# A graph network on one core: four instead of three tiles a batch gathered by matrix products in two of its passes, with the gather's table in six blocks of 128 rows and a stacked rest

## The reference

```python
def _L2_gnn_ref(inputs, timestamp, W, b, src, dst):          # pass 7
    msg = inputs[src] * timestamp
    h = jax.ops.segment_max(msg, dst, num_segments=inputs.shape[0])
    return h @ W.T + b

def _L3_gnn_ref(hx, edgefeats, edge_src, edge_dst, fnet_w1, fnet_b1, fnet_w2, fnet_b2, ...):
    w = jax.nn.relu(edgefeats @ fnet_w1 + fnet_b1) @ fnet_w2 + fnet_b2
    W = w.reshape(-1, nc, nc)
    for _ in range(NREPEATS):                                # two rounds: passes 8 and 9
        xj = hx[edge_src]
        m = jnp.einsum('ei,eio->eo', xj, W)
        agg = jax.ops.segment_sum(m, edge_dst, num_segments=n_nodes)
        agg = agg * inv_deg[:, None]
        hx = _gru_cell(agg, hx, gru_w_ih, gru_w_hh, gru_b_ih, gru_b_hh)
    return hx

x = _layernorm(x + _L0_gnn_ref(...)); x = _layernorm(x + _L1_gnn_ref(...))
x = _layernorm(x + _L2_gnn_ref(...)); x = _layernorm(x + _L3_gnn_ref(...))
```

## Time and profile before

| | |
|---|---|
| Time, median of 3 runs | 9585.77 us (9583.65 to 9609.09) |
| Profiled execution | 9624.08 us, span 9622.1 us |
| Busy over the span | PE 91%, PEld 66%, DVE 73%, ACT 38%, POOL 51% |
| Granted TensorE clock, mean | 0.915 |
| Pass 7, 8, 9 begin with the table's load at about | 4758, 6609, 8108 us |
| Indirect fetches of passes 7 to 9 (L657) | 3030, mean 970 ns |
| Products of `gather8` (L711) | 12726, mean 343 ns, overlapping |
| One-hot comparisons (L1457) | 4242, mean 316 ns |

### The profile page before, as it was taken

How to read it: one execution, slowest core, us unless ns; L and a number is a source line. 1 busy time by engine, 2 the same in 40 slices (tenths; PEclk the granted TensorE clock), 3 DMA queues, 4 the chain that set the end, 5 groups by cost and what they waited for, 6 DMA issues and landing times.

```text
span 9622.1 us, 208480 instructions
## 1 busy us (share of the span) xinstructions
PE 8789.0 (91%) x72187; PEld 6327.8 (66%) x72191; DVE 7010.4 (73%) x13550; ACT 3702.5 (38%) x10806; POOL 4954.2 (51%) x4703
## 2 busy tenths in 40 slices
PE   1599999999976999997699999998999998999998
PEld 0366666666524975976477777776777776777776
DVE  2488899999742123122378777777999998999998
ACT  5245444444320002000144444444555554555554
POOL 0588788788750000000175555544777663777662
PEclk9999999999955987987689888888999998999998
DMA  8633333333218864967732222222222221222221
GB/s 303 234 92 101 115 105 105 104 104 103 71 58 338 326 240 185 345 239 283 270 65 65 64 64 64 64 64 47 54 54 53 53 54 42 53 54 54 53 54 36
DMA packets 869111, 1162.86 MB, mean 121 GB/s; under 512 B 269846, under 2 KB 751298, under 8 KB 868118
## 3 DMA queue, kind: packets, MB, share of 16 engines
q1 hardware_dynamic: 674612, 1078.18, 33.9%
q0 software_dynamic: 150336, 28.94, 3.7%
q10 hardware_dynamic: 43426, 45.70, 1.5%
HBM read 1018.14 MB, written 133.22 MB: 120 GB/s over the span
## 4 chain that ended last, share of the span: by engine, by line
PE 66%; DVE 17%; issue 7%; DMA 5%; SPq 4%; ACT 1%; DVEq 0%; ACTq 0%
PE ps L830 16%; PE ps L711 14%; PE ps L909 9%; PE ps L700 6%; DMA arena<-adj 5%; PE ps L788 4%; PE ps L847 3%; SPq L576 3%; DVE arena L1995 3%; DVE dinv L1995 3%; PE ps L720 2%; DVE dinv L1457 2%; DVE invdeg L1457 2%; PE ps L983 2%; PE ps L795 2%
## 5 line engine op out<-in xcount | busy, mean ns | idle before, releaser
L657 POOL DMA_INDIRECT arena<-tab,x_all x3030 | 2939.7, 970 | 3700.1 <-DMA tab<-stage 2239.4
L675 POOL DMA_INDIRECT adj<-acc x1616 | 1960.8, 1213 | 560.2 <-issue 471.5
L909 PE MATMUL ps<-arena 128*128 128x192 bf16 (+1 forms) x16464 | 1167.9, 234 | 172.0 <-DMA arena<-adj 171.3
L909 PEld LDWEIGHTS ps<-arena 128*128 128x128 bf16 x16464 | 1118.2, 103 | 229.8 <-DMA arena<-adj 198.7
L711 PE MATMUL ps<-dinv,acc 112*128 112x384 bf16 x6363 | 1163.8, 342 | 44.0 <-DVE acc L1485 43.5
L1105 ACT ACTIVATE wide<-ps,not_all 128x256 bf16<-128x256 f32 x1616 | 741.0, 485 | 1197.3 <-PE ps L795 1197.3
L711 PE MATMUL ps<-invdeg,acc 112*128 112x384 bf16 x6363 | 1173.7, 344 | 2.8 <-issue 2.8
L1277 ACT ACTIVATE arena<-w_iota,rel 128x128 f32<-128x128 f32 x3232 | 988.8, 388 | 13.1
L711 PEld LDWEIGHTS ps<-dinv,acc 112*128 112x128 bf16 x6363 | 642.1, 104 | 523.7 <-issue 182.3
L711 PEld LDWEIGHTS ps<-invdeg,acc 112*128 112x128 bf16 x6363 | 645.0, 105 | 492.4 <-issue 155.4
L1621 DVE TENSOR_TENSOR arena<-hot_a,threes 128x1024 bf16<-128x1024 bf16 x606 | 738.4, 1218 | 0.0
(11 more groups left out here) (314 smaller groups left out, 14116.1 us busy)
## 6 DMA issues: line engine op xcount, KB each, us to landing
arena<-adj SPq DMA_DIRECT2D x588, 896.0 KB, 6.9
x_all<-src_parts SPq DMA_DIRECT2D x606, 192.0 KB
arena<-rels SPq DMA_DIRECT2D x202, 512.0 KB
arena<-tab SPq DMA_DIRECT2D x1616, 64.0 KB
adj<-zero SPq DMA_DIRECT2D x28, 3136.0 KB, 27.5
arena<-rT SPq DMA_DIRECT2D x404, 128.0 KB
arena<-tab,x_all POOLq DMA_INDIRECT x3030
adj<-acc POOLq DMA_INDIRECT x1616
```

The costliest lines, as they stand in the source:

```text
L657: pool.indirect_dma_start(G[b][:, u, :], None, TABLE[PHASES[p]], bass.IndirectOffsetOnAxis(ap=idx[:, t:t + 1], axis=0)).then_inc(gathered[ ...
L675: pool.indirect_dma_start(adj_cells, bass.IndirectOffsetOnAxis(ap=pair[:, t, 0:1], axis=0), pair16[:, t, 2:3], None).then_inc(celled[g], 16)
L909: last = mm(ps[:, 2 * par + u // 2, u % 2 * W:(u % 2 + 1) * W], ring[i][:, s, u * P:(u + 1) * P], rows[:, j * SC + s, :, :].rearrange("p k ...
```

## The change

In passes 8 and 9 PE gathers 4 tiles and POOL fetches 4; in pass 7 it stays at 3 and 5 (`by_pe`, `by_pool`, `skipped`, where pass 7 leaves out the first of the four tiles' columns). The table is cut into 6 blocks of 128 rows; the 16 rows left over (`LEFT`) of all three pieces are stacked at partitions 0, 32 and 64 and share one product. So `gather8` has 6 times 3 plus 1 = 19 products, of 384 columns in pass 7 and 512 in passes 8 and 9; `hot_rows` keeps 7 comparisons, now over 128 lanes, of 384 or 512 columns. The table's load is one DMA plus three small ones, and the cut has two more small copies on DVE. `src_parts` and its broadcast loads grow from 3 to 4 tiles in all three passes. Line numbers in the diff are not the profile's.

```diff
-GT = 3
+GT = 4
-FETCHED = HT - GT
-BLANES = NB8 // BL
+BLANES = P
+LAST = BL - 1
+LEFT = NB8 - LAST * BLANES
+STACKED = 3 * 32
+def by_pe(p, k):
+    return GT - 1 if p == 7 else GT
+def by_pool(p, k):
+    return HT - by_pe(p, k)
+def skipped(p, k):
+    return GT - by_pe(p, k)
...
# SyncE, start of a pass
-                sp.dma_start(x8_whole, tab_blocks).then_inc(x8_in, 16)
+                sp.dma_start(x8_whole[:, 0:LAST, :], tab_blocks).then_inc(x8_in, 16)
+                if p == 7:
+                    sp.wait_ge(left_open, 1)
+                for i in range(3):
+                    sp.dma_start(x8_whole[32 * i:32 * i + LEFT, LAST, :], tab_left).then_inc(x8_in, 16)
...
# POOL, gather_rows
-                for u in range(FETCHED):
+                for u in range(by_pool(p, k)):
...
# PE, gather8
-                for b in range(BL):
+                lo = skipped(p, j) * P
+                for b in range(LAST):
                     for i in range(3):
-                        last = mm(picked_rows, x8[:, b, i, :], hot8[j % 2][:, b, :],
-                                  start=b == i == 0, stop=b == BL - 1 and i == 2)
+                        mm(picked_rows[:, lo:], x8[:, b, i, :], hot8[j % 2][:, b, lo:], start=b == i == 0, stop=False)
+                last = mm(picked_rows[:, lo:], x8[0:STACKED, LAST, 0, :], hot8[j % 2][0:STACKED, LAST, lo:],
+                          start=False, stop=True)
...
# PE, turn8
-                for u in range(GT):
+                for u in range(skipped(p, j), GT):
...
# DVE, hot_rows
+                lo = skipped(p, j) * P
                 for b in range(BL):
-                    last = ts(hot8[j % 2][:, b, :], parts_row[j % SL][0:BLANES, 0:GC], lane_b[0:BLANES, b:b + 1], None,
+                    last = ts(hot8[j % 2][:, b, lo:], parts_row[j % SL][0:BLANES, lo:GC], lane_b[0:BLANES, b:b + 1], None,
                               ALU.is_equal)
...
# DVE, select8
-                stt(picked_by[j % 2], parts_row[j % SL][:, GC:], lane_a[:, 0:1], picked_rows, ALU.is_equal, ALU.mult
+                lo = skipped(p, j) * P
+                stt(picked_by[j % 2][:, lo:], parts_row[j % SL][:, GC + lo:], lane_a[:, 0:1], picked_rows[:, lo:],
+                    ALU.is_equal, ALU.mult
...
# DVE, open_select
+                dve.wait_ge(x8_cut, at + 4)
+                for i in (1, 2):
+                    nc.vector.tensor_copy(x8[32 * i:32 * i + 32, LAST, 0, :], x8[32 * i:32 * i + 32, LAST, i, :]
+                                          ).then_inc(x8_cut, 1)
```

More of the change, by code:

```diff
@@ L172, in build @@
         hot8 = [(dinv if i == 0 else invdeg)[0:BLANES, o:o + BL * GC // 2].bitcast(bf16).rearrange("p (b e) -> p b e", b=BL)
-                for i, o in enumerate((HOT8, 5120))]
+                for i, o in enumerate((HOT8, 4864))]
         src_g, src_t = [x_all[0:T // TR, 1664 + i * 2 * GC:1664 + (i + 1) * 2 * GC].bitcast(i32) for i in range(2)]
         src_16 = [x_all[0:T // TR, 1664 + (4 + i) * GC:1664 + (5 + i) * GC].bitcast(f16) for i in range(2)]
-        PARTS0 = 1664 + 6 * GC
+        PARTS0 = 1664
         parts_row = [x_all[:, PARTS0 + i * GC:PARTS0 + (i + 1) * GC].bitcast(f16) for i in range(SL)]
-        CONST0 = PARTS0 + SL * GC
+        CONST0 = 1664 + 6 * GC
         lane_b, lane_a = x_all[:, CONST0:CONST0 + BL], x_all[:, CONST0 + 8:CONST0 + 9]
@@ L280, in build @@
         src_parts = nc.dram_tensor("src_parts", [T // HT, 2, GC], f16).ap()
-        tab_blocks = tab16.rearrange("(b l a) f -> l b (a f)", b=BL, a=A8)
+        tab_blocks = tab16[0:LAST * BLANES * A8, :].rearrange("(b l a) f -> l b (a f)", b=LAST, a=A8)
+        tab_left = tab16[LAST * BLANES * A8:NB8 * A8, :].rearrange("(l a) f -> l (a f)", a=A8)
         dst_tiles = a["dst_r"].rearrange("o (t e) -> (o t) e", e=P)
@@ L318, in build @@
         x8_cut = sem("x8_cut")
+        left_open = sem("left_open")
         hot8_made, picked, selected, turned, copied = [{p: sem(f"{x}{p}") for p in range(7, NPASS)}
@@ L368, in build @@
         PARTED = 9
-        BIAS_CUT = 13
+        BIAS_CUT = 14
         def tables(n):
@@ L381, in gather_count @@
             s = k % len(G)
-            return 16 * FETCHED * ((p - 7) * len(range(s, NB, len(G))) + k // len(G) + 1)
+            whole = sum(by_pool(q, b) for q in range(7, p) for b in range(s, NB, len(G)))
+            return 16 * (whole + sum(by_pool(p, b) for b in range(s, k + 1, len(G))))
         def part_count(p, j):
@@ L724, in open_gather @@
             def open_gather(p):
-                pe.wait_ge(x8_cut, 4 * (p - 6))
+                pe.wait_ge(x8_cut, 6 * (p - 6))
                 gather8(p, 0)
@@ L1300, in cut8 @@
             def cut8(p):
-                act.wait_ge(x8_in, 16 * (p - 6))
+                act.wait_ge(x8_in, 64 * (p - 6))
                 act_fn(x8[:, :, 0, :], x8_whole, ACT.Copy).then_inc(x8_cut, 1)
-                act.wait_ge(x8_cut, 4 * (p - 7) + 2)
+                act.wait_ge(x8_cut, 6 * (p - 7) + 2)
                 act_fn(x8[:, :, 1, :], x8_rest, ACT.Copy).then_inc(x8_cut, 1)
@@ L1311, in copy8 @@
                 act.wait_ge(turned[p], j + 1)
-                act_fn(G[j % len(G)][:, FETCHED:, :], turned_rows.rearrange("p (u f) -> p u f", f=16),
+                act_fn(G[j % len(G)][:, by_pool(p, j):, :],
+                       turned_rows[:, skipped(p, j) * 16:].rearrange("p (u f) -> p u f", f=16),
                        ACT.Copy).then_inc(copied[p], 1)
@@ L1449, in cut_bias @@
                     stt(bias3, bias_piece, is_row[:, 2:3], bias3, ALU.mult, ALU.add).then_inc(bias_cut, 1)
+                    dve.wait_ge(parted, PARTED)
+                    ts(lane_b[:, LAST:BL], strip_row[:, :], float(LAST * BLANES), None, ALU.add).then_inc(bias_cut, 1)
             def hot_rows(p, j):
@@ L1478, in open_select @@
                 dve.wait_ge(parted, PARTED)
+                dve.wait_ge(bias_cut, BIAS_CUT)
                 hot_rows(p, 0)
-                at = 4 * (p - 7)
-                dve.wait_ge(x8_in, 16 * (p - 6))
+                at = 6 * (p - 7)
+                dve.wait_ge(x8_in, 64 * (p - 6))
                 dve.wait_ge(x8_cut, at + 1)
@@ L1913, in _ @@
             dve.wait_ge(consts_in, 16 * CONSTS)
+            nc.vector.memset(x8_whole[:, LAST, :], 0.0).then_inc(left_open, 1)
             dve.wait_ge(acc_packed, 16 * GR)
@@ L1992, in messages8 @@
                         dve.wait_ge(ten[p].sem, ten[p].at(k, WT8))
-                        if q == FETCHED // 2:
+                        if q == by_pool(p, k) // 2:
                             dve.wait_ge(copied[p], k + 1)
```

2 lines of the change are left out of this document (1 added, 1 removed).

## The result

| | before | after |
|---|---|---|
| Time, median of 3 runs (lowest to highest) | 9585.77 us (9583.65 to 9609.09) | 9861.92 us (9850.36 to 9864.09) |
| Profiled execution | 9624.08 us | 9850.36 us |
| Pass 7, 8, 9 | 1829.9, 1474.1, 1476.7 us | 1698.0, 1651.7, 1651.8 us |
| Mean batch of pass 7, 8, 9 | 8.88, 7.13, 7.13 us | 8.24, 8.00, 8.00 us |

A forecast was written before the change was run, and what follows sets the result against it. It took DVE to bound passes 8 and 9, and PE pass 7. Its terms, -81 + 2 x (129 + 5.9) = +189 us, took the profiled 9624 to 9813; for the median 9774 us, range 9655 to 9850.

The forecast's parts named there:

- So DVE sets the pace, and PE has 7.11 - 0.34 = 6.77 us of work: Pass 8 before the change: DVE never idles, PE waits 0.34 us a batch at `turn8` and can take on 0.33.
- The loop through both: Passes 8 and 9: the chain of waits through PE and DVE sets the batch, 7.76 us, taken as 7.75, +0.65.
- A product of 512 columns, 0.216 us: Passes 8 and 9 on PE: cost goes by columns, 19 products take 4.10 us, +0.70 a batch.
- Rival A: Passes 8 and 9: wide products cost what 384 columns do, DVE stays the bound; +73, 9659 us, chance 0.07.
- Two more in `turn8`: Passes 8 and 9 on PE: two more matmuls in `turn8`, where six take 0.70 us, add 0.23 a batch.
- DVE's own 7.48: Passes 8 and 9: DVE's own work a batch in us, with +0.23 for seven comparisons and +0.15 for `select8`.
- Openings, +5.9 each: Start of a four-tile pass: more DMA issues, copies, a costlier first gather and three more gathers, together +5.9 us.
- POOL's silence has no effect: Passes 8 and 9: POOL is no bound, its share of pass 8 falls to about 50% and gives DVE nothing.
- Rival D: Passes 8 and 9: fetches hold DVE without an idle row; chance 0.04 with whatever else makes it faster.
- Pass 7, -81: Pass 7 on PE: two products fewer, 0.40 us a batch over 202 batches, -81 us (ends -66 and -131).
- Rival C: Pass 7 loses its half-clock batches: -259 us there, +11 in all, 9597 us, chance 0.06.
- Rival B: PE's clock drops in passes 8 and 9 too: batch 8.69 us, +561, 10147 us, chance 0.05.

The follow-up runs named there:

- five comparisons: Passes 8 and 9 with five of the seven comparisons: on the changed kernel 9844.67 us, on the kernel before 9584.07 us.
- gather first: Changed kernel with `gather8` ahead of `turn8` in PE's order of passes 8 and 9: 10205.11 us.
- the version with three tiles: Changed kernel with three tiles by PE in all passes (19 products of 384 columns, 5 fetches): 9471.82 us, 0.9889 of before; on another chip 9468.30, 0.9859.
- two-tile version: The version with three tiles, but in pass 7 two tiles on PE and 6 fetched: 9471.56 us, 0.9890 of before.

## Why the prediction came out as it did

- **"So DVE sets the pace, and PE has 7.11 - 0.34 = 6.77 us of work": this is the step that failed.** The 0.34 was read in the row of the weight loads, with `select8` as releaser 0.05 behind its end, and taken for idle time of PE. PE's products waited for DVE 1.3 us in all of pass 8, and its busy time of over 99% said the same. 0.22 of the gap was the last group of strip products at work and 0.11 PE's own delay behind them; the gap is there whether or not `select8` is done (five comparisons) and moves with the strips' end (gather first). PE's own batch was 7.09 us, and it could take on nothing. With that, the prediction's own terms give 7.10 + 0.70 + 0.23 = 8.03; with the 0.21 that `turn8` really added it is 8.00, as measured. Against the mean of 7.13 that is 8.003 - 7.127 = +0.876 in each of 198 batches, 173 us, and with the opening 178 and 175 a pass, where the prediction had 135.
- **The loop through both** was summed rightly (7.80 with the measured terms, against 7.76) and never decided here, being under PE's 8.00. That the same sum gave today's 7.10 was no test of it: its terms were read from the batch that it was to give. On the one odd chip it does decide.
- **A product of 512 columns, 0.216 us:** right (0.216 in the trace, 0.214 by two more). Rival A is out, and with it the Trainium skill's figure ("TensorE: Matmul & The Clock Gate", Back-to-back issue gap) of about 131 ns for a load and product of 512 columns: no run here shows one under 214. **Two more in `turn8`,** +0.23: 0.91 against 0.70, +0.21.
- **DVE's own 7.48** was short: it is 8.00 - 0.36 = 7.64 in the changed kernel. Seven comparisons took 1.97 us (7456.24 + 2.40 to 7460.62), not 1.83: in the trace six of them start 0.26 apart, as summed, but the fifth takes 0.41 in every batch, for a reason that stays open. It cost nothing, since DVE waits.
- **Openings, +5.9 each:** from the table's load (L565, in the change L585) to the first L1057 of the pass it is 34.7 and 32.9 us instead of 30.0 and 29.8, so +4.7 and +3.1.
- **POOL's silence has no effect:** right, 47% of pass 8, and nothing faster. Rival D is out.
- **Pass 7, -81:** the batch at full clock is 7.61 us, as summed, but 132 us went. The sum counted two products and left the clock alone; the wider table (112 to 128 rows) had an effect of its own, 90 us by the run that has it alone. From there to the changed kernel it is 26 to 42 us more, under the 64 of two products at full clock (0.32 times 198); with differences of 32 us between executions of one code this split is rough. Rival C was the right direction, half its size, and its reason against, that the stretch without gather products is as long as before, missed that what fills the burst counts too.
- **Rival B** didn't come (clock 1.00 in pass 8), but it was a real one: the one execution with `turn8` and `gather8` swapped has it, with 387 us of pass 8 at half clock. In pass 7 busy time alone doesn't tell the clock: before and its copy over 128 rows are busy for 1632.01 and 1630.06 of 1634 us, at 0.89 and 0.94. The Trainium skill (same page, Part 1) ties the throttle to how busy PE has been; by these two runs it also matters what PE does while it is busy.
- **The balance:** +83 too little in passes 8 and 9, 51 too little gained in pass 7, 6 more ahead of pass 7: 189 - 51 + 83 + 6 makes 227. That the medians lie 276 apart and not 226 is the profiled executions: before's was 38 us above its median and the changed one's 12 below.

## What to carry to other kernels

When two engines stand at the same pace, a wait of one on the other proves nothing: take work off the engine that is named as releaser and see whether the gap goes; only what goes is slack. And look for PE's slack in the row of its products, not in that of its weight loads: there the 0.34 of each batch was 1.3 us in a whole pass, while the version with three tiles, which does wait, shows 41.3. It may also pay to widen a table's rows to fill the array before taking products away: here it left the products' time as it was and gave 58 to 90 us of clock (on the odd chip a third of a per cent in all), while the fewer, thinner products of the two-tile version gave all they saved back to the clock.

## What the runs showed of the hardware that was not expected

- Between the products over 32-row strips, four side by side, and `turn8` over all 128 rows PE loses 0.11 us (1.19 less five times 0.216), in both kernels; behind products over all rows nothing (0.86 for four).
- 21 products over 128 rows instead of 112 take the same time and leave 244 us of pass 7 at half clock instead of 429.
- With two groups of instructions on PE in the other order, and the same ones in each batch, the clock of pass 8 was 0.90 instead of 1.00 (one execution).
- In one job of four the step from the start of PE's strip products to DVE's multiplication took 3.02 us instead of 1.43, the clock of the kernel before fell to 0.87 in pass 8, and a change that costs 2.6% elsewhere gained 2.6%.
